# Two gated attention layers on one core: the order of loads and first steps in the kernel's opening

## The reference

```python
h = layernorm(x) * g_in
q = h @ Wq                      # 512 -> 1024: 16 heads of 64
k, v = split(h @ Wkv)           # 512 -> 128: one k and one v of 64, shared by all heads
k, v = [null_k; k], [null_v; v] # a null key and value in front
s = scale(q, k) + bias + null column; causal and key mask
o = softmax(s) @ v
x = x + layernorm(o @ Wo) * g_out
```

## Time and profile before

| | |
|---|---|
| runs | 1288.45, 1288.96, 1290.61 us; median 1288.96 |
| profiled execution | 1289.25 us; span of its trace 1287.4 us |
| TensorE (PE) | 1251.4 us busy, 97% of the span |
| VectorE (DVE) | 1116.7 us, 87% |
| ScalarE (ACT) | 824.6 us, 64% |
| GpSimd (POOL) | 806.8 us, 63% |

### The profile page before, as it was taken

The page is one execution under the profiler, slowest core; times in us unless marked ns, Lnnn a source line. Parts: engine busy times, 40 slices in busy tenths (PEclk is TensorE's granted clock), DMA queues, the critical chain, the costliest instruction groups (busy, mean ns, idle before and its releaser), DMA issues.

```text
span 1287.4 us, 28691 instructions
## 1 busy us (share of the span) xinstructions
PE 1251.4 (97%) x8456; PEld 1158.1 (90%) x8456; DVE 1116.7 (87%) x2872; ACT 824.6 (64%) x3154; POOL 806.8 (63%) x1382
## 2 busy tenths in 40 slices
PE   5899999999999999999999999999999999999997
PEld 5899998998999999998899999999999999999995
DVE  6788988988888888887899899999998999999986
ACT  4756665665666765666666666766666667666673
POOL 6645444545447866557576766766667667676673
PEclk9999999999999999999999999999999999999998
DMA  8320101110622321326440101101101011011101
GB/s 206 118 70 31 50 26 50 51 50 26 99 66 99 124 99 51 116 71 208 140 175 32 50 24 49 49 24 49 39 35 49 24 49 49 24 49 37 37 34 42
DMA packets 52220, 85.99 MB, mean 67 GB/s; under 512 B 7888, under 2 KB 22256, under 8 KB 51616
## 3 DMA queue, kind: packets, MB, share of 16 engines
q1 hardware_dynamic: 46880, 75.02, 18.7%
q0 software_dynamic: 4128, 9.03, 2.5%
q10 hardware_dynamic: 1120, 0.82, 0.2%
HBM read 57.07 MB, written 27.79 MB: 66 GB/s over the span
## 4 chain that ended last, share of the span: by engine, by line
PE 86%; DVE 6%; issue 3%; POOL 2%; ACT 2%; DMA 1%; SPq 1%; POOLq 0%; DVEq 0%; ACTq 0%
PE bank_y L1808 26%; PE bank_q L1726 16%; PE bank_s L1628 12%; PE bank_o L1628 10%; PE bank_q L1628 9%; PE bank_p L1773 6%; PE bank_t L1669 2%; PE bank_t L1741 2%; PE bank_t L1628 1%; DVE v_l L1395 1%; ACT p_raw L987 1%; DMA bias<-in_fside_16xSxS 1%; DVE pt_l L1431 1%; DVE ot_l L1437 1%; DVE v_l L1392 1%
## 5 line engine op out<-in xcount | busy, mean ns | idle before, releaser
L987 ACT ACTIVATE p_raw<-s_sb,neg_m 128x130 f32<-128x130 f32 (+1 forms) x1024 | 371.8, 366 | 170.1 <-DVE neg_m L1421 165.4
L756 POOL TENSOR_TENSOR p_sb<-p_raw,rden 128x256 f32<-128x256 f32 x256 | 159.4, 623 | 230.2 <-DVE rden L1427 229.9
L1808 PE MATMUL bank_y<-wo_h,ot_h 128*128 128x512 f32 x512 | 218.4, 426 | 1.0 <-DVE ot_l L1437 1.0
L746 POOL TENSOR_TENSOR bias_g<-bias,mask_row 128x260 f32<-128x260 f32 x256 | 179.7, 702 | 62.1 <-DVE s_sb L1414 61.2
L1808 PE MATMUL bank_y<-wo_h,ot_l 128*128 128x512 f32 x512 | 202.9, 396 | 0.0
L1808 PE MATMUL bank_y<-wo_l,ot_h 128*128 128x512 f32 x512 | 202.9, 396 | 0.0
L987 ACT ACTIVATION_READ_ACCUMULATOR p_raw<-s_sb,neg_m 128x1 f32 x1024 | 193.2, 189 | 0.0
L1431 DVE TENSOR_TENSOR pt_l<-bank_p,pt_h 128x384 fp32r<-128x384 f32 x256 | 140.8, 550 | 41.9 <-ACT pt_h L994 41.8
L994 ACT ACTIVATE pt_h<-bank_p 128x384 fp32r<-128x384 f32 x256 | 123.4, 482 | 54.7 <-PE bank_p L1773 54.2
L1628 PE MATMUL bank_q<-xt_h,wq_h 128*128 128x256 f32 x512 | 150.1, 293 | 1.7 <-DVE xt_l L1302 1.7
L1414 DVE TENSOR_TENSOR s_sb<-bank_s,bias_g 128x392 f32<-128x392 f32 x256 | 141.7, 554 | 7.4 <-ACT p_raw L987 5.4
(11 more groups left out here) (165 smaller groups left out, 3611.6 us busy)
## 6 DMA issues: line engine op xcount, KB each, us to landing
x_res<-in_x SPq DMA_DIRECT2D x32, 256.0 KB, 2.9
x_mid<-y_out SPq DMA_DIRECT2D x32, 256.0 KB, 2.0
x_in<-x_mid SPq DMA_DIRECT2D x32, 256.0 KB, 2.8
x_res<-x_mid SPq DMA_DIRECT2D x32, 256.0 KB, 2.7
out_x<-y_out SPq DMA_DIRECT2D x32, 256.0 KB, 2.0
x_in<-in_x SPq DMA_DIRECT2D x30, 256.0 KB, 3.3
wq_raw<-in_L_cond_Wq SPq DMA_DIRECT2D x4, 768.0 KB, 6.6
wq_store<-w_sb SPq DMA_DIRECT2D x6, 384.0 KB, 4.0
```

Source lines behind the costliest of these rows:

```text
L746: e.tensor_tensor(low_blocks(to), low_blocks(of), mask_row[:, :].unsqueeze(1).broadcast_to([P, 2, LOW]), ALU.add)
L756: e.tensor_tensor(to[:, 0:2 * P].rearrange("p (e j) -> p e j", e=2), low_blocks(of)[:, :, 2:LOW], r[:, 0:2, :].broadcast_to([P, 2, P]), AL ...
L987: last = e.activation(p_raw[:, g % 2, lo:hi], s_sb[:, g % 2, lo:hi], ACT.Exp, bias=neg_m[:, h:h + 1], accum_out=esum[:, h:h + 1])
L1808: last = e.matmul(bank_y[:, :], a[:, c, :], b[:, c, :], start=(c == 0 and k == 0), stop=(c == OC - 1 and k == 2))
```

## The change

- SyncE asks for x of item 1 as its second load, ahead of all weights; ScalarE's queue no longer does. Of the bias it loads only the first half (`pair` 0, four loads); GpSimd issues the other four behind its first reciprocal deviations and ahead of the ten small loads. A semaphore `pool_loaded` counts these four and the two of the null bias, and `place_nulls(0)` waits for all six.
- GpSimd makes the bias of group 0 ahead of item 2's deviations, and of the others likewise; in the first `pair` it makes two `normalise` of item 1 ahead of the `start_output` that stood in front of them.
- ScalarE and VectorE split query weights of part 0 in two halves, with the splits of both transposed x between; the null key comes ahead of the first `ln_apply`.
- VectorE takes the last part of the query weights and item 2's and 3's x out of the opening, into a new `first_scores` for item 0, and so does TensorE with item 2's transposes.
- TensorE makes 24 transposes of the identity ahead of the first x and 8 ahead of the first products, into a bank that the scores write later; its first projections wait for the weights chunk by chunk.
- What is computed stays the same.

```diff
@@ SyncE
             load_x((0, 0))
+            e.dma_start(x_res[:, :], x[1]).then_inc(x1_loaded, 16)
             load_wq(0, 0)
             load_wkv(0)
             for p in (1, 2):
                 load_wq(0, p)
             e.dma_start(x_out, x[2]).then_inc(x2_loaded, 16)
-            for pair_rows in range(2):
-                load_bias0(pair_rows)
+            load_bias0(e, 0, bias0_loaded)
             wait(e, xn_ready, (0, 0))
@@ GpSimd, mask_bias0
-                    e.wait_ge(bias0_loaded, 16 * BIAS_LOADS)
+                    e.wait_ge(bias0_loaded, 16 * BIAS_LOADS // 2)
@@ GpSimd, pair
-                on(0, start_output, 4)
                 on(1, normalise, 0)
                 on(1, low_part, 0)
+                on(1, normalise, 1)
+                on(0, start_output, 4)
+                on(1, normalise, 2)
                 on(0, start_output, 6)
-                on(1, normalise, 1)
-                on(1, normalise, 2)
@@ GpSimd, opening
             inverse_deviations(1)
+            load_bias0(e, 1, pool_loaded)
             load_small()
-            e.wait_ge(null_bias_loaded, 16 * LAYERS)
+            e.wait_ge(pool_loaded, 16 * POOL_LOADS)
             place_nulls(0)
-            inverse_deviations(2)
             mask_bias0(0)
             masked_bias((0, 0), 0)
+            inverse_deviations(2)
             mask_bias0(1)
             masked_bias((0, 0), 1)
+            inverse_deviations(3)
             mask_bias0(2)
+            masked_bias((0, 0), 2)
             mask_bias0(3)
-            inverse_deviations(3)
-            masked_bias((0, 0), 2)
@@ ScalarE, opening
-            query_weights(0)
+            query_weights(0, range(2))
             split_xt(first)
             split_xt(second)
+            query_weights(0, range(2, KC))
             key_weights()
             query_weights(1)
             split_group(first, 0)
             split_keys(first)
-            copy_values(first)
             query_weights(2)
             split_group(first, 1)
+            copy_values(first)
@@ VectorE, in front of pair
+            def first_scores(at):
+
+                m = at(0)
+                scores(m, 0)
+                maxima(m, 0)
+                ln_apply(at(2))
+                split_group(m, 1)
+                x_stats(at(3))
+                means_variances(3, [at(3)], [])
+                scores(m, 1)
+                maxima(m, 1)
+                query_weights(2)
+                sums(m, 0)
+                split_group(m, 2)
+                ln_apply(at(3))
+                values_back(m)
+                scores(m, 2)
+                split_group(m, 3)
+                split_xt(at(2))
@@ TensorE, project_group
-                if is_item(m, 0, 0):
-                    for p in ((0,), (0, 1), (1,), (2,))[g]:
-                        e.wait_ge(wq_ready[p], KC)
...
+                        if is_item(m, 0, 0) and r == 0:
+                            for p in ((0,), (0, 1), (1,), (2,))[g]:
+                                e.wait_ge(wq_ready[p], c + 1)
@@ TensorE, opening and first scores
+            def warm(n):
+
+                for k in range(n):
+                    e.transpose(bank_s[0][:, 0:P], ident[:, :], ident[:, :])
+
+            def first_scores(at):
+
+                m = at(0)
+                scores(m, 0)
+                transpose_x(at(2))
+                project_group(m, 2)
+                scores(m, 1)
+                transpose_v(m)
+                project_group(m, 3)
+
             first = (0, 0)
+            warm(24)
             transpose_x(first)
             transpose_x((0, 1))
+            warm(8)
             project_group(first, 0)
             project_kv(first)
-            transpose_x((0, 2))
             project_group(first, 1)
```

More of the change, by code:

```diff
@@ L408, in pieces, with low_and_up, load_bias0 @@
             return [(c, wo_raw[:, c, :], high[:, j % 2, k, :]) for k, c in enumerate((c0, c0 + 1))]
+        def low_and_up(layer, pair):
+            rows = slice(pair * HALF, (pair + 1) * HALF)
+            groups = bias[rows, layer, :, :]
+            low = groups[:, :, 0:LOWS].rearrange("p g (e j) -> p g e j", e=2)[:, :, :, 2:LOW]
+            up = groups[:, :, LOWS:GW].rearrange("p g (e j) -> p g e j", e=2)[:, :, :, 2:UP]
+            return low, up
+        def load_bias0(e, pair, loaded):
+            heads = bias0.rearrange("(g r e) i j -> r i g e j", g=G, r=2)
+            low, up = low_and_up(0, pair)
+            for k in range(2):
+                e.dma_start(low[:, :, k, :], heads[pair, HALF:P, :, k, :]).then_inc(loaded, 16)
+                e.dma_start(up[:, :, k, :], heads[pair, 0:HALF, :, k, 0:HALF]).then_inc(loaded, 16)
         def batch_of(m):
@@ L461, in store @@
                 e.dma_start(out_of[m[0]][m[1]], x_out).then_inc(x_stored, 16)
[L463 to L476, removed]
             def load_mask(layer):
@@ L1165, in second_null, with weights @@
                 e.wait_ge(nk_step, 6)
-            def weights(columns, h_ready, ready):
-                for c in range(KC):
+            def weights(columns, h_ready, ready, chunks):
+                for c in chunks:
                     e.wait_ge(h_ready, c + 1)
@@ L1681, in project_group @@
                     features = slice((2 * g + r) * P, (2 * g + r + 1) * P)
-                    passes = []
                     for c in range(KC):
+                        if is_item(m, 0, 0) and r == 0:
+                            for p in ((0,), (0, 1), (1,), (2,))[g]:
+                                e.wait_ge(wq_ready[p], c + 1)
                         xh, xl = (t[:, c, :].rearrange("p (a u i) -> p a u i", a=2, u=2) for t in (xt_h, xt_l))
                         wh, wl = (t[:, c, features] for t in (wq_h, wq_l))
-                        passes += [(wh, xh), (wh, xl), (wl, xh)]
-                    last = product(out[:, r, :, :, :], passes)
+                        for k, (w, t) in enumerate(((wh, xh), (wh, xl), (wl, xh))):
+                            last = e.matmul(out[:, r, :, :, :], w, t, start=(c == 0 and k == 0),
+                                            stop=(c == KC - 1 and k == 2))
                 last.then_inc(g_psum[g], 1)
@@ L1847, in on @@
                         stage(at(d), *which)
-                on(0, scores, 0)
-                on(0, scores, 1)
                 if is_item(at(0), 0, 0):
-                    project_group(at(0), 2)
-                    transpose_v(at(0))
-                    project_group(at(0), 3)
+                    first_scores(at)
+                else:
+                    on(0, scores, 0)
+                    on(0, scores, 1)
                 on(-1, attend, 1)
```

65 lines of the change are left out of this document (29 added, 36 removed).

## The result

The changed kernel takes 1294.5 us (median of 6 runs, 1293.25 to 1295.49), the kernel before, run beside it, 1289.11. The ratio is 1.0035, 95% interval 1.0024 to 1.0046: slower. The profiled execution's span went from 1287.4 to 1292.5 us, 5.1 more. The page's first part of the changed kernel, against the earlier trace rows, doesn't tell where it comes from: TensorE has 6.3 us more on record, about what the 32 identity transposes take (4.70 and 1.92 us), its share is the same 97%, and the other engines differ by 1 us at most.

A forecast was written before the change was run, and what follows sets the result against it. TensorE, busy 97%, leaves only the opening to change, where the bias wait and item 4's x count: 24.35 + 11.1 + 13.9 − 44.48 − 0.5 = +4.4 us on 1289.25, as median 1293.4; 8-in-10 range 1287 to 1298.

The forecast's parts named there:

- The low parts behind the second scores: VectorE's four low parts of the last query weights now hang on R; their end moves from 25.21 to 35.45 us.
- The row of steps from R to W: First scores, item 2's normalisation, transposes, group 2's products, second scores, low parts: 11.1 us, ends 9.2 and 13.4.
- R: Moment the first scores may take their bias: 24.93 us before, forecast 24.35, ends 21.75 and 24.95.
- W: Moment all four low parts of the last query weights are done: 25.21 us before, forecast 35.45.
- The bias by two queues: Four bias loads each on SyncE and GpSimd: SyncE's last lands at 21.5 us instead of 22.1, giving R 24.35.
- x of item 1 on SyncE's queue: 256 KB ahead of the weights in the opening: costed at nothing, as the first scores wait for R anyway.
- The halving: Bias split over two queues: SyncE's half lands at 21.5 us; landing at 22.1 would make the sum 0.6 larger.
- Rival 3: GpSimd's bias half lands last: R 27.7 us, sum +7.7, time 1296.7; chance 0.15.
- W to x of item 4: SyncE from W through Wo to item 4's x landing: 13.9 us as before, landing at 49.35 instead of 39.1.
- The credit for GpSimd's order: Low parts of Wo behind two normalisations, easing TensorE's 2.03 us wait and low clock: 0.5 us, ends 0 and 3.7.
- Identity transposes: 24 and 8 on TensorE in the opening: at most 32 × 0.27 us on an idle engine, cost nothing.
- the main term: Low parts of the last query weights behind the first two scores, so W follows R by 11.1 us.

The follow-up runs named there:

- e1: The changed kernel with VectorE's four low parts of the last query weights ahead of the first scores instead of behind the second: 1290.78 us, ratio 1.0013.
- e7: The kernel before with only the four low parts of the last query weights moved behind the second scores and maxima: 1292.83 us, ratio 1.0027.
- e5: The changed kernel with x of item 1 issued by ScalarE's queue again instead of SyncE's: 1291.9 us, ratio 1.0012.
- e6: The changed kernel with item 2's deviations and normalisation ahead of the first masked bias and first scores: 1291.82 us, ratio 1.0019.
- e3: The changed kernel with all eight bias loads on SyncE's queue again, none on GpSimd: 1293.89 us, ratio 1.0045.
- e11: e8 with all eight bias loads on SyncE's queue again: 1284.86 us, ratio 0.9965.
- e2: The changed kernel with SyncE asking for item 4's x ahead of Wo, w1 and g_out: 1294.83 us, ratio 1.0044.
- e9: The changed kernel without the 24 and 8 identity transposes: 1293.44 us, ratio 1.0034.
- e4: The kernel before with GpSimd's low part pairs of Wo moved behind one and two normalisations of item 1: 1288.03 us, ratio 0.9995.
- e8: The changed kernel with x of item 1 by ScalarE, item 2's normalisation early, and the low parts directly behind it: 1285.05 us, ratio 0.9961.
- e12: e8 with null key late, last query weights behind the bias half, their low parts behind second scores, item 4's x ahead of Wo: 1287.68 us, ratio 0.9985.

## Why the prediction was right, and where it wasn't

The forecast was 1293.4, in a range from 1287 to 1298, slower; measured 1294.5. Point by point:

- **The low parts behind the second scores.** Right. The row of steps from R to W was forecast at 11.1 us and took 11.06: first scores and maxima 1.2, normalisation 0.8, transposes and products 5.35 (forecast 5.5, at the low clock for two thirds of the products, as forecast), scores 0.85, second scores and maxima 1.1, low parts 1.66 (1.8). e1 (3.7 us less) and e7 (3.5 us more than before) show that this part makes about two thirds of the loss. The shares don't add up: e5 and e6 take 2.6 and 2.7 us off as well, and all three together 9.4.
- **The bias by two queues.** R was off by 1.9 us (26.27 for 24.35), beyond my upper end of 24.95. The step that failed is the one that cost x of item 1 on SyncE's queue at nothing: I looked at the weights behind it and not at the bias at the end of the same queue. e5 shows it at 2.6 us of the time and 2.5 of R. From the occupied DMA engines I had also concluded that the issue isn't what is slow; in e5 against the changed kernel the landing moves with the issue (9.20 instead of 11.36). The halving was credited with 0.6 us; e3 and e11 show none (21.7 on one queue, 22.0 on two). The Trainium skill ("DMA: Bandwidth & Descriptors", section "Issuing engines are not separate DMA queues") says that loads started by different engines interleave on the same 16 DMA engines, so that several issuers save no more than issue time. These two landings agree with it; by it I should have gone. Rival 3, GpSimd's half last, did not come: it landed at 20.3.
- **W to x of item 4.** 14.6 us measured against 13.9, right as a duration, but its two parts moved against each other: 5.8 us to the issue and 8.1 to the landing before, 2.3 and 12.2 in the changed kernel. In the kernel before the load's issue at 31.04 came with the end of item 3's normalisation, which I had not read there:

```profile
30.10 0.91 DVE L1297 TENSOR_SCALAR xn<-x_in,mean_var,rstd 128x512 f32<-128x512 f32 x1 [2.23 <-POOL rstd L775]
```

  The landing was 13.8 us behind Wo's issue before, 14.4 in the changed kernel and 14.0 in e7. I take it that the bytes of Wo and of what follows it are what carries over, and not SyncE's steps; no run tries this alone. As the only path it was wrong: VectorE waited for the load, 2.59 us, but without that wait its statistics would have come at 49.3, 4.8 us later than before. e2 removed the load from the path and gained nothing (with R 1.0 us later in its profile), e7 lost its 3.5 us without a wait for the load. Group 3's products, which need the same low parts, are the second path, and I had left them out.
- **The credit for GpSimd's order.** Mis-sized: item 4's statistics are 7.4 us late and the end is 5.1 to 5.4, so 2.0 to 2.3 us came back behind it where I had put 0.5. The low clock from 56 to 60 us stayed in the changed kernel's profile (0.59), behind a wait of 2.72 us instead of the 2.03; e3 and e9, which have GpSimd's order too, show 1.00 there, behind waits of 2.5 and 2.0. e4 alone puts the order at 1.3 us or nothing (its interval holds both). How the rest comes back is not settled.
- **Identity transposes.** At nothing, right (e9), with the clock raised earlier and lowered again before group 2, as argued.

So the sum's errors are R, 1.9 us too early, W to x of item 4, 0.7 too short, and the credit, 1.5 to 1.8 too small. The last is opposite to the others. The direction and the main term were reasoned; that the forecast is 1.1 us from the result, nearer than its parts, is luck.

## What to carry to other kernels

Of a step that is moved behind a wait, list all that stands behind its result, not the first consumer only: here a transfer through a reused buffer and a group of products, in e7 0.4 us apart, so that removing one can show nothing. A load that was put second in a queue went with a last load 2.1 to 2.5 us later here, so look at the end of the queue for what is waited for. And raising TensorE's clock ahead of a wait of several microseconds bought nothing here: with the wait cut from 5.62 to 2.19 us (e6, item 2's transposes and group 2's products in it) or to 1.3 (e8) the clock stayed; with 2.70 (e5) it fell.

## What was not expected of the hardware

- Issuing is not of fixed length: the third bias load took SyncE 0.86 us in e5 and 3.4 us in the changed kernel, 4.7 in e3, and in e5 the fourth took 2.3. In each of these three a load asked for between 7.9 and 9.2 us is a long one.
- The same short wait of TensorE has two outcomes. After 1.66 or 1.67 us of idle time ahead of group 3's products these ran at 0.12 us each in the changed kernel, e3 and e9 (granted clock 1.00) and at 0.21 in e2 and e5 (0.66). After 1.85 us they ran slow in e6 and e12, after 2.64 in e7. What decides between the two at the same wait these runs don't show; it is about 2.2 us.
- VectorE's four low parts of 256 columns took 1.66 us beside an idle GpSimd (changed kernel) and 2.65 to 2.92 beside its masks (e6, e8, e12, before). That GpSimd is the reason is inferred from the overlap; no run changes it alone.
